# Layer norm of the row tiles moved to ScalarE, a fourth staging buffer, VectorE's order rearranged, and the graph groups spread four and three to a tile with 21 in the query stage

## The reference: one graph transformer layer

```python
xn = ln(x)
W  = zeros(1024, 1024).at[src, dst].add(edge_weight)     # 41250 edges, entries beyond 1023 dropped
g  = xn @ W.T + gnn_bias                                 # graph part
q, k, v = split(xn @ W_qkv, 3)                           # 1024 x 3072
q, k = relu(rms(q) * qn_w), relu(rms(k) * kn_w)
kv = einsum('nhd,nhe->hde', k, v); ks = k.sum(rows)      # 16 heads of 64
a  = (q @ kv) / (q . ks + eps)
x1 = x + g + a @ W_out + b_out
y  = x1 + moe(rms(ln(x1)) * scale)                       # 8 experts, top 2, swiglu, hidden 256
```

## Time and profile before

| | us |
|---|---|
| median of 3 runs | 1065.67 (1064.27 to 1067.94) |
| the profiled execution | 1066.02 |
| its span | 1064.3 |
| PE busy | 942.8 |
| DVE busy | 730.8 |
| ACT busy | 300.7 |

### The profile page before, as it was taken

The page is one execution under the profiler, slowest core; times in us unless marked ns, Lnnn a source line. Parts: engine busy times, 40 slices in busy tenths (PEclk is TensorE's granted clock), DMA queues, the critical chain, the costliest instruction groups (busy, mean ns, idle before and its releaser), DMA issues.

```text
span 1064.3 us, 16221 instructions
## 1 busy us (share of the span) xinstructions
PE 942.8 (89%) x5425; PEld 586.6 (55%) x5426; DVE 730.8 (69%) x1216; ACT 300.7 (28%) x517; POOL 173.4 (16%) x210
## 2 busy tenths in 40 slices
PE   3797889988889899999999999999719999999992
PEld 2465556666566566555566666666615445455551
DVE  5666988898988899536876777775365555555551
ACT  3435333323233111433111222221103333233331
POOL 1000000000000000000432332321212323333321
PEclk9898999999999999999999999999759999999997
DMA  9753456655454410792015555556719987977543
GB/s 291 195 184 100 150 159 187 196 159 175 147 173 142 162 34 21 179 338 57 21 59 168 160 159 155 163 155 178 266 40 343 300 243 203 316 202 190 118 86 59
DMA packets 89161, 176.58 MB, mean 166 GB/s; under 512 B 24824, under 2 KB 39160, under 8 KB 89088
## 3 DMA queue, kind: packets, MB, share of 16 engines
q1 hardware_dynamic: 81328, 147.50, 44.8%
q0 software_dynamic: 7776, 28.32, 11.9%
HBM read 113.63 MB, written 62.67 MB: 166 GB/s over the span
## 4 chain that ended last, share of the span: by engine, by line
PE 34%; DVE 31%; DMA 17%; ACT 5%; issue 5%; POOL 3%; SPq 3%; DVEq 1%; POOLq 0%; ACTq 0%
PE windows L1032 10%; DMA arena<-in_w_flat 8%; PE bank L906 6%; PE bank L1050 4%; DMA arena<-t_dram,arena 4%; DVE arena L1449 3%; DVE arena L1456 3%; DVE arena L1610 3%; PE bank L938 2%; PE bank L1023 2%; PE bank L932 2%; POOL arena L657 2%; PE bank L760 2%; DVE arena L1436 2%; DVE arena L1434 2%
## 5 line engine op out<-in xcount | busy, mean ns | idle before, releaser
L760 PE MATMUL bank<-arena 128*125 128x512 f16 x960 | 218.6, 385 | 21.8 <-DVE arena L1422 12.8
L760 PEld LDWEIGHTS bank<-arena 128*125 128x125 f16 x960 | 131.0, 139 | 97.2 <-issue 12.3
L1032 PE MATMUL windows<-arena 128*128 x648 | 149.3, 380 | 0.0
L906 PE MATMUL bank<-arena 128*128 128x416 f16 (+1 forms) x576 | 107.4, 342 | 1.8 <-DMA arena<-split_dram 1.8
L932 PE MATMUL bank<-arena 128*125 128x512 f16 x432 | 97.5, 383 | 4.1 <-DVE arena L1646 2.5
L1032 PEld LDWEIGHTS windows<-arena 128*128 128x128 f16 x648 | 63.6, 98 | 65.4 <-issue 1.0
L938 PE MATMUL bank<-arena 128*125 128x512 f16 x432 | 97.5, 384 | 0.0
L906 PEld LDWEIGHTS bank<-arena 128*128 128x128 f16 x576 | 55.6, 98 | 46.5 <-issue 2.4
L932 PEld LDWEIGHTS bank<-arena 128*125 128x125 f16 x432 | 59.4, 138 | 38.8 <-issue 3.5
L938 PEld LDWEIGHTS bank<-arena 128*125 128x125 f16 x432 | 59.7, 138 | 34.3 <-issue 1.5
L1672 DVE SCALAR_TENSOR_TENSOR arena<-arena 128x512 f16<-128x512 f32 x40 | 40.2, 1005 | 55.6 <-ACT arena L1268 55.4
(11 more groups left out here) (237 smaller groups left out, 1433.1 us busy)
## 6 DMA issues: line engine op xcount, KB each, us to landing
arena<-split_dram SPq DMA_DIRECT2D x56, 512.0 KB, 5.4
arena<-in_w_flat SPq DMA_DIRECT2D x44, 512.0 KB, 4.9
split_dram<-arena SPq DMA_DIRECT2D x88, 256.0 KB, 2.8
arena<-in_w_flat SPq DMA_DIRECT2D x40, 256.0 KB, 4.2
split_dram<-arena SPq DMA_DIRECT2D x80, 128.0 KB, 2.4
arena<-in_x SPq DMA_DIRECT2D x20, 448.0 KB
arena<-in_w_qkv SPq DMA_DIRECT2D x8, 1024.0 KB, 10.6
t_dram<-arena SPq DMA_DIRECT2D x10, 448.0 KB
```

The source lines that it names most:

```text
L760: mm = pe.matmul(bank[b][0:TT, :], xt[:, l, k, tok(i)], wkv[:, r, k, c0:c0 + 512], start=(k == 0 and n == 0), stop=(k == KT - 1 and n == 2))
L906: mm = pe.matmul(bank[u % 3][:, 0:n], wq[h][:, l, k, :], xt[:, r, k, a:a + n], start=(k == 0 and c == 0), stop=(k == KT - 1 and c == 2))
L1032: mm = pe.matmul(bank[6][:, :], rowT[s][:, l, k, :], arena16[:, bass.ds(off + (r * KT + k) * 512, 512)], start=(k == 0 and c == 0), stop=( ...
```

## The change

- Tile 0 keeps the old norm. Tiles 1 to 9 are normed on ScalarE: `row_sums` (a copy with a row sum, a scale of the sum, two squares with row sums, each waiting for the one before), `row_root`, `row_norm`; VectorE keeps three instructions of one column (`row_variance`, `row_scale`).
- The key and value weights get a fourth staging buffer, which lies on the places of row tiles 2 and 3; those tiles and tile 4 are loaded after the last part is split.
- `k_half` is divided in two on both engines, with a piece between; `make` is divided from `accumulate`; `first_counts` and `window_counts` (edge table) move back behind the first `kv_sums` and the first `v_half`s.
- Graph groups: 4 and 3 in turn per tile (28), 21 in the query stage over 13 units; `FIRST_SPLIT` is 13; `load_wq(2, 1)` goes ahead of the 16 stores.
- Pieces: 4 in tile 1, 5 in each of the others; ScalarE does the first of the next tile's pieces at the end of a tile.

```diff
-KV_GROUPS = 4 * (NT - 2)
+GROUPS_OF = [0, 0] + [4, 3] * (NT // 2 - 1)
+KV_GROUPS = sum(GROUPS_OF)
-        wide = [view(one_hot_at, [PIECE]), view(stage_at, [PIECE]), view(B_AT, [PIECE])]
+        wide = [view(one_hot_at, [PIECE]), view(stage_at, [PIECE]), view(B_AT, [PIECE]), view(xs_late_at, [PIECE])]
-        HALVES_OF = [0, 6, 5, 5, 5, 5, 5, 5, 4, 4]
+        HALVES_OF = [0, 4] + [5] * (NT - 2)
-        for u in range(11):
-            if u in (1, 3, 5, 7, 9, 10):
+        for u in range(13):
+            if u % 3 > 0:
-        FIRST_SPLIT = 11
+        FIRST_SPLIT = 13
...
@@ sync @@
-                if m >= 3:
-                    sp.wait_ge(wkv_lo, m - 2)
+                if m >= 4:
+                    sp.wait_ge(wkv_lo, m - 3)
-            load_wkv(3)
-            load_wkv(4)
-            load_x(2)
-            load_wkv(5)
-            load_x(3)
-            for m in (6, 7):
+            for m in range(3, KT):
                 load_wkv(m)
-            load_x(4)
+            sp.wait_ge(wkv_lo, KT)
+            for i in (2, 3, 4):
+                load_x(i)
...
             load_wq(2, 0)
+            load_wq(2, 1)
...
-                if k == 3:
-                    load_wq(2, 1)
@@ scalar @@
+            def row_sums(i):
+                b, st_ = i % 4, row_st[0:TT, i % 2, :]
+                a_.wait_ge(x_in[b], 32 * (i // 4 + 1))
+                a_.activation(xs[b][0:TT], xs[b][0:TT], ACT.Copy, accum_out=st_[:, 0:1]).then_inc(row_sum, 1)
+                a_.wait_ge(row_sum, i)
+                a_.activation(st_[:, 1:2], st_[:, 0:1], ACT.Copy, scale=-1.0 / D).then_inc(row_mean, 1)
+                a_.wait_ge(row_mean, i)
+                for half in range(2):
+                    if half == 1:
+                        a_.wait_ge(row_sq, 2 * i - 1)
+                    a_.activation(junk[0:TT], xs[b][0:TT, half * 512:half * 512 + 512], ACT.Square, bias=st_[:, 1:2],
+                                  accum_out=st_[:, 2 + half:3 + half]).then_inc(row_sq, 1)
+            def row_root(i):
+                a_.wait_ge(row_var, i)
+                a_.activation(st_[:, 5:6], st_[:, 4:5], ACT.Sqrt, bias=eps_x[0:TT], scale=1.0 / (D * SX * SX)).then_inc(row_sd, 1)
+            def row_norm(i):
+                a_.wait_ge(row_rs, i)
+                a_.activation(xs[b][0:TT], xs[b][0:TT], ACT.Identity, bias=st_[:, 7:8], scale=st_[:, 6:7]).then_inc(xn_ready, 1)
+            def k_relu(i, c):
                 a_.wait_ge(kw_ready, 2 * i + c + 1)
+                a_.wait_ge(kv_used, START + i)
...
             for i in range(2, NT):
-                k_half(i, 0)
-                piece_hi(hs[0])
-                k_half(i, 1)
+                k_square(i, 0)
+                k_relu(i, 0)
+                piece_hi(hs[1])
+                if i + 2 < NT:
+                    row_sums(i + 2)
+                    a_.wait_ge(row_sq, 2 * (i + 2))
+                k_square(i, 1)
+                k_relu(i, 1)
                 k_root(i)
-                piece_hi(hs[1])
+                if i + 2 < NT:
+                    row_root(i + 2)
                 xt_hi_half(i + 1, 0)
+                piece_hi(hs[2])
                 v_half(i, 0)
-                piece_hi(hs[2])
                 xt_hi_half(i + 1, 1)
                 piece_hi(hs[3])
-                    ln_sqrt(i + 2)
+                    row_norm(i + 2)
                 v_half(i, 1)
-                for m in hs[4:]:
-                    piece_hi(m)
+                piece_hi(hs[4])
+                if i + 1 < NT:
+                    piece_hi(halves(i + 1)[0])
@@ vector: the loop after the change @@
+                k_weighted(i, 0)
+                piece_lo(hs[0])
+                k_low(i, 0)
+                accumulate(n)
+                make(n + 2)
+                    row_variance(i + 2)
+                k_weighted(i, 1)
+                k_sum()
+                piece_lo(hs[1])
+                k_low(i, 1)
+                accumulate(n + 1)
+                norm_of_k(i)
+                    row_scale(i + 2)
+                    xt_lo_half(i + 1, 0)
+                make(n + 3)
+                piece_lo(hs[2])
+                v_half(i, 0)
+                accumulate(n + 2)
+                    xt_lo_half(i + 1, 1)
+                make(n + 4)
+                piece_lo(hs[3])
+                v_half(i, 1)
+                if GROUPS_OF[i] == 4:
+                    accumulate(n + 3)
+                    make(n + 5)
+                piece_lo(hs[4])
```

More of the change, by code:

```diff
@@ L798, in _ @@
             kv_unit(0, 0, 0)
-            first_counts()
             pe.wait_ge(wkv_lo, 4)
@@ L819, in _ @@
             kv_sums()
+            first_counts()
+            kv_unit(1, 1, 512)
+            pe.wait_ge(xn_ready, 2)
+            pe.wait_ge(kw_ready, 3)
+            xt_half(2, 0)
             pe.wait_ge(table_step, 2)
@@ L838, in _ @@
             for i in range(2, NT):
-                n = 4 * (i - 2)
+                n = sum(GROUPS_OF[0:i])
                 pe.wait_ge(xt_done, 2 * i + 2)
@@ L1131, in _ @@
                 wkv_part_hi(m)
-            ln_sqrt(1)
-            for m in (3, 4):
-                wkv_part_hi(m)
-            k_half(0, 0)
-            for m in (5, 6):
-                wkv_part_hi(m)
-            k_half(0, 1)
+            row_sums(1)
+            wkv_part_hi(3)
+            row_root(1)
+            wkv_part_hi(4)
+            row_norm(1)
+            k_square(0, 0)
+            wkv_part_hi(5)
+            k_relu(0, 0)
+            wkv_part_hi(6)
+            k_square(0, 1)
             wkv_part_hi(7)
+            k_relu(0, 1)
             k_root(0)
-            ln_sqrt(2)
             for half in range(2):
@@ L1480, in _ @@
                 xt_lo_half(0, half)
-            wkv_part_lo(1)
-            stats(1)
-            wkv_part_lo(2)
-            norm(1)
-            window_counts()
-            for m in (3, 4):
+            for m in (1, 2):
                 wkv_part_lo(m)
+            row_variance(1)
+            wkv_part_lo(3)
+            row_scale(1)
+            wkv_part_lo(4)
             v.wait_ge(knw_in, 16)
-            k_half(0, 0)
-            for m in (5, 6):
-                wkv_part_lo(m)
-            k_half(0, 1)
+            k_weighted(0, 0)
@@ L1493, in _ @@
+            wkv_part_lo(5)
+            k_low(0, 0)
+            wkv_part_lo(6)
+            k_weighted(0, 1)
+            k_sum()
             wkv_part_lo(7)
+            k_low(0, 1)
             norm_of_k(0)
-            stats(2)
             for half in range(2):
                 xt_lo_half(1, half)
-            norm(2)
             for c in range(2):
                 v_half(0, c)
+            window_counts()
+            row_variance(2)
+            row_scale(2)
+            k_weighted(1, 0)
@@ L1501, in _ @@
+            k_low(1, 0)
             window_picks()
+            row_variance(3)
             hs = halves(1)
-            for n in hs[0:2]:
-                piece_lo(n)
-            v.wait_ge(kv_used, START + 1)
-            k_half(1, 0)
+            k_weighted(1, 1)
+            k_sum()
+            piece_lo(hs[0])
+            k_low(1, 1)
+            norm_of_k(1)
+            row_scale(3)
+            xt_lo_half(2, 0)
+            piece_lo(hs[1])
             read_windows()
+            v_half(1, 0)
@@ L1550, in _ @@
                 v_half(i, 1)
-                accumulate(n + 3)
-                for m in hs[4:]:
-                    piece_lo(m)
+                if GROUPS_OF[i] == 4:
+                    accumulate(n + 3)
+                    make(n + 5)
+                piece_lo(hs[4])
             v.wait_ge(qn_in, 16)
@@ L1616, in q_turn @@
                         if (6 * t + u, at) in Q_AT:
-                            accumulate(Q_AT[6 * t + u, at])
+                            accumulate_make(Q_AT[6 * t + u, at])
                     if last and u >= 4:
```

150 lines of the change are left out of this document (76 added, 74 removed).

## The result

The changed kernel takes 1053.08 us (median of 4 runs, 1050.46 to 1055.8) against 1065.33 before: a ratio of 0.9882 with a 95% interval of 0.9851 to 0.9912, 12.3 us faster. The forecast was 1057 in a range of 1036 to 1065. The profiled span is 1051.2 against 1064.3.

A forecast was written before the change was run, and what follows sets the result against it. The loop's pace was taken to be set by a ring of piece buffers through VectorE, SyncE and ScalarE, with VectorE and TensorE near full. Terms -11.5 - 6.0 - 3.5 + 12 + 0 = -9.0 from 1066.0 gave 1057.0, range 1036 to 1065.

The forecast's parts named there:

- Start, -11.5: Start up to tile 2's keys: fourth buffer and later tile loads bring the weights sooner; -11.5 us, between -6 and -16.
- The ring, -6.0: Loop, tiles 2 to 8: buffer cycle from piece's end through store, load and ScalarE to next keys; 218.9 against 224.9 us.
- Alternating turns: Sign in the loop: turns of 30.5 and 32.5 us in alternation, with ScalarE idle before a piece and a tile's first square.
- late sums: Loop: row sums behind piece 1's late data make VectorE wait 2.6 us after a four-group tile, 0.6 after a three-group one.
- End of the loop, -3.5: From tile 9's keys to the first query unit: tile 9 loses a group, 17.2 us for 20.7; -3.5.
- Query groups, +12: Query stage up to its last group: four more groups and two more units cost +12 us, 11 to 15.7.
- Last group to folds, 0: Query stage's end: six units, then TensorE idles 10 us for the output weights; 37.0 against 36.9, -3 to +3.
- the two units' 8.4 us: Behind the last group: the 8.4 us of two units moved forward are lost in a stall before the folds.
- A: Rival in the loop: row sums hidden on ScalarE, turn 29.9 us in every tile, total 1047; chance 0.20.
- B: Rival in the loop: TensorE is the bound, its work 195.6 us for seven tiles, total 1034; chance 0.09.
- C: Rival in the loop: data for the piece ahead of the square land late, ring longer; at 2.5 us, 1074; chance 0.12.
- D: Rival on ScalarE: identity needs another function table, two loads for each of nine tiles, 23 us; 1065; chance 0.03.

The follow-up runs named there:

- experiment 3: Changed kernel with three staging buffers for the key and value weights and the old order of loads: 1060.82 us, ratio 0.9956 to the kernel before.
- experiment 5: Changed kernel loading only 128 of 1024 columns from the fifth half piece on (weights written back not the reference's): 1038.52 us, ratio 0.9749.
- experiment 2: Changed kernel with ScalarE's first half piece of a tile taken behind the square and relu of its first keys: 1052.57 us, ratio 0.9870.
- Experiments 7: Changed kernel with three of four loads of the output weights' low half issued at the start of the query stage: 1050.67 us, ratio 0.9847.
- experiment 9: Changed kernel with unit 18's query weights issued among the 16 accumulator stores, after the sixth: 1058.53 us, ratio 0.9918.
- experiment 10: Changed kernel with unit 18's query weights among the stores and three quarters of the output weights' low half loaded early: 1051.61 us, ratio 0.9866.
- experiment 4: Changed kernel with four graph groups in every tile and 17 in the query stage over 11 units: 1043.41 us, ratio 0.9787.
- experiment 6: Changed kernel with ScalarE's row sums moved behind the first value half, VectorE's two small norm steps after them: 1046.01 us, ratio 0.9804.
- experiment 12: Changed kernel with four groups per tile, row sums behind the first value half, and the fourth piece ahead of the one-hots: 1031.41 us, ratio 0.9669.
- experiment 1: Changed kernel with the norm of tiles 1 to 9 given back to VectorE, the root on ScalarE: 1057.44 us, ratio 0.9918.

## Why the prediction was right, and where it was off

The total, 1057 against 1053, is closer than its terms: the loop beat its term by 7.3 and the query groups missed theirs by 3.8, the other way. That these errors partly cancel is luck.

*Start, -11.5: right.* -12.6, and experiment 3 gives most of it to the loads. The low halves' end (39) and the block at 40 were met within 0.5. One input was off without harm: in the first 8 us of the kernel before 1.7 MB moved, not 2.2.

*The ring, -6.0: mechanism right, size off.* Alternating turns were seen (28.4, 32.3, 30.3, 32.8, 28.6, 31.7, 27.7 for 30.5 and 32.5), with idle ahead of the piece and of the second square, and experiment 5 shows that with the data there sooner the loop comes down to TensorE's work. The pace was mis-sized in three places. VectorE's order from keys to the end of piece 3 was put at 21.7; it is 21.06 (89.48 to 110.54), and tiles 3 to 7 have the same 21.06 plus their wait for the sums, 4.5 less in seven turns. From the end of that piece to the next keys I took 8.2, with 5.5 for the data; it is 6.9 to 7.9, with the data 4.4 to 5.4 after the ask, some 5 less in seven. So a turn without late sums is 28.4 (tile 2) and not 29.9. The late sums were put at 0.6 and 2.6 a tile, 9.6 in all; second keys less 6.07 give 3.6, 1.9, 3.8, 0, 2.8, 12.1 in all, 2.5 more. Together that is, within 0.4, the 7.3 by which the loop beat the forecast. One sign was not met: TensorE was to idle 3 to 5 us a tile, and it idles 12.5 in the whole loop of eight tiles, 1.6 each. And the two waits hand on what they lose, which the turn's sum doesn't show: built on the ring alone, my expectation for experiment 2 had a gain of 6 to 10 for taking the piece away from the first square, and there was none.

*End of the loop, -3.5: right.* -3.3.

*Query groups, +12: too small.* 15.8, at the upper bound that VectorE's work alone gave. The 2 to 3 us that I took off for VectorE entering the stage less late were not there: the stage took 93.9 to 94.2 in all ten kernels with 21 groups, however the loop ahead of it ran. Neither engine is the bound alone: two groups in one unit are VectorE's 3.67 apart and TensorE waits for them (5.9 us in seven waits), and in the units with one group VectorE waits 0.7 to 1.6 for TensorE.

*Last group to folds, 0: the size near, the cause half right.* 34.5 for 37.0, an idle of 7.0 for 10. I named the output weights, whose chain was to end at 35.5; the folds do wait for them, but only 0.93, while 6.03 of the idle stand before unit 18, which I had waiting for nothing. Experiments 7, 9 and 10 show two transfers side by side, the query weights of unit 18 behind 16 stores in SyncE's order, and the output weights behind the stores' landing. The remark that the two units' 8.4 us are lost in a stall was right, and experiment 4 puts the whole move of the groups at +9.7.

*Rivals.* A (sums hidden, 1047) is about what experiment 6 made of it, 1046, with second keys 6.0 to 8.0 after the first. B (TensorE the bound, 1034) is reached by experiment 12, with four groups in every tile. C and D did not happen: the data of the piece ahead of the keys were there 4.4 to 5.4 after the ask, and there is still one table load up to 325 us, in the start:

```profile
L1107 ACT ACTIVATE arena<-arena 125x512 f16<-125x512 f32 x18 | 13.0, 722 | 0.6
...
L1118 ACT ACTIVATE arena<-arena 125x1024 f32<-125x1024 f32 x9 | 11.1, 1230 | 0.4 <-DVE arena L1461 0.4
L1100 ACT ACTIVATE arena<-arena 125x1024 f32<-125x1024 f32 x9 | 9.4, 1044 | 0.0
...
L1087 ACT ACT_TABLE_LOAD x1 | 1.3, 1283 | 0.9 <-PEq L1960 0.9
```

These are the changed kernel's groups by line up to 325 us; L1118 is the norm with identity, L1100 and L1107 are the copy and the squares of the row sums. The Trainium skill ("ScalarE: Activation LUTs", Table sets: the hidden batching unit) has identity in every set, and the trace with its one load agrees. By the rule of the Trainium skill ("ScalarE: Activation LUTs", Rules for kernel authors) the norm would stay on VectorE. For the single instruction the trace agrees: 1.23 on ScalarE against 0.81 on VectorE. For the kernel it did not decide: with the norm on VectorE (experiment 1) it was 4.4 slower by the medians, and 11.4 slower than with the sums at a better place (experiment 6); ScalarE is busy 96.7 of the 211.6 us from tile 2's keys to tile 9's, VectorE 173.2.

## What to carry to other kernels

When a loop's two busiest engines are each about 90% busy and neither is full, follow one buffer round: from the instruction that frees it over the queue that asks for it to the engine that waits for it in order, and add that up; here that sum met the turns of 30 us within 1 us on the average. Look for the next wait in the same order before moving the first: moved alone, the late piece only changed the instruction that waited for it (experiment 2, no gain), while taking the sums from behind it gave 7.1 (experiment 6). Experiment 2's edit was not run together with the others, so whether it gains once the sums are moved is open. Work that seems free to move may be the cover of a transfer: ask what it hides where it stands, before it is put elsewhere to relieve a loop (experiment 4, 9.7). And when several edits go in together, put each back alone: the norm's move, named first in the title, was worth 1.6 of the loop's 13.3 as its sums then stood.

## What the runs showed of the hardware

After an idle of 6.03 us TensorE ran a unit of 24 matmuls in 6.29 us, at a mean granted clock of 0.69, where a unit takes 4.4 at 1.00. After an idle of 10.38 (experiment 9) it ran six fold matmuls in 2.72 and the next unit in 6.05, at mean granted clocks of 0.50 (the lower level, 1.2 GHz) and 0.72, against 1.46 and 4.4 at 1.00. After one of 5.66 (experiment 10) it was 2.72 and 4.53. So the price of an idle was 1.9, 2.9 and 1.4 us in these three profiles, and joining two idles into one of 10.4 did not make it cheaper than the 1.9 after the first of the two.

A ScalarE pass over 125x1024 with scale and bias from columns took 1.23 us, a copy of it 1.04, a square of 512 with a bias column 0.72; reading a row sum out is an instruction of its own, 0.19. Sixteen stores of 256 KB kept SyncE's queue for 14.5 us, 0.9 each, and the load behind them in its order was issued only then.
